# A graph kernel whose table entries are loaded as addresses without a range check at run time

## What is computed

```python
def reference(x, src, dst, edge_attr_4, edge_attr_8, ...):
    # layer 0: attention over the edges (4 heads of 64), plus one self-loop for each node
    h = (x @ W).reshape(N, H, C)
    e = leaky_relu(a_src[src] + a_dst[dst])
    alpha = exp(e - segment_max(e, dst)[dst]);  alpha /= segment_sum(alpha, dst)[dst]
    x = layernorm(x + elu(segment_sum(h[src] * alpha, dst) + bias + x @ skip_W))
    # layer 1: weights w from a three-layer MLP of edge_attr_8; reads at dst, sums into src
    w = mlp(edge_attr_8)                       # 256 values an edge
    mid_s, mid_v = products(w, ys[dst], yv[dst], edge_attr_4)
    ns, nv = segment_sum(mid_s, src), segment_sum(mid_v, src)   # scaled by rsqrt(degree)
    return layernorm(x + rms_normed(ns @ w2_s + sc_s, nv @ w2_v + sc_v))
```

## Time and profile before

| | |
|---|---|
| device time, median of 3 runs | 8239.94 us (8227.58 to 8246.67) |
| span of the profiled execution | 7531.3 us |
| device time of the profiled execution itself | not recorded; the timed median is 708.6 us above the span |
| TensorE busy (matmuls) | 6552.1 us, 87% |
| GpSimd busy | 5759.5 us, 76% |
| VectorE busy | 5437.6 us, 72% |
| ScalarE busy | 4022.4 us, 53% |
| mean granted TensorE clock | 0.988 |
| instructions, sequencers' among them | 218435 |
| instruction queues' DMA packets | 13 and 28 |

### The profile page before, as it was taken

The page is one execution under the profiler, slowest core; times in us unless marked ns, Lnnn a source line. Parts: engine busy times, 40 slices in busy tenths (PEclk is TensorE's granted clock), DMA queues, the critical chain, the costliest instruction groups (busy, mean ns, idle before and its releaser), DMA issues.

```text
span 7531.3 us, 218435 instructions
## 1 busy us (share of the span) xinstructions
PE 6552.1 (87%) x36547; PEld 4301.1 (57%) x36548; DVE 5437.6 (72%) x20339; ACT 4022.4 (53%) x12733; POOL 5759.5 (76%) x4888
## 2 busy tenths in 40 slices
PE   6999999999999988888888888888888888888876
PEld 5666666666666555555555555555555555555544
DVE  3788888888888798666666666666666666666668
ACT  2455555555555455555555555555555555555532
POOL 3677777777777655888888888888888888888878
PEclk8899999999999999999999999999999999999999
DMA  5788888888888766777777777777777777777789
GB/s 178 200 224 223 224 225 224 222 224 226 224 223 223 207 221 192 136 136 135 136 135 135 136 136 136 136 135 136 135 135 137 136 136 135 136 136 135 136 227 299
DMA packets 1268411, 1312.20 MB, mean 174 GB/s; under 512 B 232303, under 2 KB 1153040, under 8 KB 1268272
## 3 DMA queue, kind: packets, MB, share of 16 engines
q0 software_dynamic: 368112, 577.39, 45.5%
q1 hardware_dynamic: 900258, 734.36, 33.8%
HBM read 723.28 MB, written 587.78 MB: 174 GB/s over the span
## 4 chain that ended last, share of the span: by engine, by line
PE 38%; issue 23%; POOL 19%; DMA 8%; DVE 7%; POOLq 2%; ACT 2%; DVEq 1%; ACTq 0%; SPq 0%
POOL part L571 13%; PE PS L845 12%; PE PS L837 12%; DMA part<-arena,c_idx 8%; POOL d_out L562 5%; PE PS L866 3%; PE PS L862 2%; PE PS L959 2%; PE PS L952 1%; PE PS L878 1%; ACT arena L724 1%; DVE arena L1310 1%; PE PS L871 1%; PE PS L789 1%; DVE arena L1298 1%
## 5 line engine op out<-in xcount | busy, mean ns | idle before, releaser
L571 POOL DMA_INDIRECT part<-arena,c_idx x1664 | 2671.4, 1605 | 515.8 <-issue 457.7
L522 POOL DMA_INDIRECT arena<-h_tab,sidx x1664 | 1773.8, 1066 | 634.9 <-issue 385.7
L1279 DVE SCALAR_TENSOR_TENSOR arena<-PS,c_src,lower_eq 128x128 f32<-128x128 f32 x1664 | 517.6, 348 | 1385.1 <-PE PS L964 1385.1
L717 ACT COPY arena<-PS 128x514 f32<-128x514 f32 x832 | 489.7, 589 | 1823.5 <-DMA part<-arena,c_idx 1823.3
L952 PE MATMUL PS<-ident,arena 128*128 128x128 f32 x3328 | 545.1, 286 | 679.7 <-ACT arena L724 666.5
L921 PEld LDWEIGHTS PS<-ident,arena 128*128 128x128 f32 x6656 | 739.8, 141 | 626.9 <-issue 582.7
L562 POOL DMA_INDIRECT d_out<-y_tab,c_row x832 | 829.2, 997 | 266.6 <-issue 252.6
L921 PE MATMUL PS<-ident,arena 128*128 128x128 f32 x6656 | 977.0, 280 | 61.5 <-issue 43.0
L710 ACT COPY arena<-PS 128x512 f32<-128x512 f32 x1664 | 991.7, 603 | 6.8 <-PE PS L921 6.7
L1157 DVE TENSOR_TENSOR big<-big,PS 128x260 f32 x1664 | 703.9, 423 | 396.2 <-PE PS L845 336.1
L845 PE MATMUL PS<-arena 128*128 128x260 f32 x3328 | 961.4, 412 | 3.5 <-DVE big L1157 2.2
(11 more groups left out here) (192 smaller groups left out, 11545.7 us busy)
## 6 DMA issues: line engine op xcount, KB each, us to landing
w_tab<-arena SPq DMA_DIRECT2D x416, 520.0 KB
arena<-w_tab SPq DMA_DIRECT2D x1664, 130.0 KB
part<-zeros SPq DMA_DIRECT2D x1664, 32.1 KB
arena<-part SPq DMA_DIRECT2D x392, 128.5 KB, 3.4
arena<-h_tab,sidx POOLq DMA_INDIRECT x1664
ot_tab<-arena SPq DMA_DIRECT2D x416, 64.0 KB
arena<-ot_tab SPq DMA_DIRECT2D x416, 64.0 KB
part<-arena,c_idx POOLq DMA_INDIRECT x1664
```

The source lines that it names most:

```text
L522: pool.indirect_dma_start(hg[:, s, k, :], None, h_tab, bass.IndirectOffsetOnAxis(ap=sidx[:, s, k:k + 1], axis=0)).then_inc(s_hg[s], 16)
L571: pool.indirect_dma_start(part[q], bass.IndirectOffsetOnAxis(ap=c_idx[:, s, k:k + 1], axis=0), o_cmb[:, q, :], None, compute_op=ALU.add).t ...
```

## The change

`numbers` passes an argument that leaves out the run-time check of each loaded entry against its range. The two rows are clamped from below too, at 0, in the same two VectorE instructions that clamped them from above. Nothing else changes; the other loads with a range (the flag `wide`, and the entry in the loop that runs only where it is set) keep their checks.

```diff
+        IN_RANGE = "both rows are clamped to their range where they are built"
...
         def numbers(eng, row, at, n, below):
 
             return nc.values_load_multi_w_load_instructions(row[:, ds(at, n)], engines=(eng.engine,), min_val=0,
-                                                            max_val=below - 1)[1]
+                                                            max_val=below - 1,
+                                                            skip_runtime_bounds_check_because=IN_RANGE)[1]
...
             flat = PS[:, 0:4, :].rearrange("p b n -> p (b n)")[:, 0:T]
-            v.tensor_scalar(block_row, flat[0:1, :], float(NB - 1), None, ALU.min)
+            v.tensor_scalar(block_row, flat[0:1, :], float(NB - 1), 0.0, ALU.min, ALU.max)
             link(v.tensor_tensor(iota_t[32:33, :], flat[32:33, :], iota_t[32:33, :], ALU.add))
-            v.tensor_scalar(window_row, iota_t[32:33, :], float(EW - 1), None, ALU.min)
+            v.tensor_scalar(window_row, iota_t[32:33, :], float(EW - 1), 0.0, ALU.min, ALU.max)
```

## The result

The kernel after takes 8365.1 us (median of 4 runs, 8346.3 to 8392.6), the kernel before 8233.8 us on the same chip (4 runs, 8210.1 to 8246.7, the shown ones among them): a ratio of 1.017 with an interval of [1.0138, 1.0203]. It is slower, by some 131 us. The forecast was no change, 8239 us, and the range ended at 8275 us.

A forecast was written before the change was run, and what follows sets the result against it. The prediction took TensorE to bound stage A and GpSimd's scatters and gathers stage C. Its terms, four of 0, then -0.7 and +0.4, gave -0.3 us on 8239.94: 8239 us, range 8210 to 8275.

The forecast's parts named there:

- The sum: Whole kernel: all parts add to -0.3 us, set against the timed median 8239.94 us; the 708.6 us taken as untouched.
- Parts 1 and 2: Stage A: dropping TensorE's and VectorE's checks, 4 a step each, gains 0, as TensorE sets the pace.
- Part 2: Stage A, VectorE's 4 checks a step: 0.34 us idle before L1168, up to 141 us of room; gain 0.
- Part 3: Stage C, TensorE's checks in every second step: 0.28 us earlier, 116 us in all, then waiting for L724; gain 0.
- the rival priced at 116 us: Stage C: TensorE sets the pace, so 0.28 us comes out of each of 416 pairs, 8124 us; chance 0.07.
- the scatters get dearer: Stage C: SyncE's earlier loads raise one scatter in four to 1700 ns, +40 us, 8280 us; chance 0.08.
- Parts 4 and 5: SyncE's checks in stage C gain 0 directly; starts of stages A and C gain 0.7 us once, 0.5 at C.
- Part 6: The two clamps: a second operation costs 0 to 0.86 us once, taken as 0.4 us.

The follow-up runs named there:

- e16: Kernel before, unchanged, profiled in series 7 (late kind): 8213.1 us in one run, beside 8201.4 us for before.
- series 6: Late set of runs: before 8190.3 us; after with one added TensorE wait 8138.9 us (0.9949); after unchanged 8324.8 us (1.0162).
- e4: Kernel after, unchanged, run again in the prompt kind on another chip: 7526.0 us against 7529.9 us for before (1.0002).
- series 7: Late set of runs: before 8201.4 us; checks dropped only for TensorE's stage A loads 1.0054; checks kept only there 1.0177.
- series 4: Late set of runs: before 8261.4 us; after 0.9988; checks dropped only for TensorE's stage A loads 0.9958; kept only there 1.0003.
- e8: Kernel before, unchanged, in series 4 (late kind): before takes 8261.4 us there.
- e18: Kernel before with clamps and all checks dropped except those of TensorE's stage A loads, in series 7: 8381.6 us (1.0177).
- series 3: Late set of runs: before 8252.4 us; scatters cut to 64 of 128 rows, with checks 8036.0 us, without checks 7981.7 us.

## Why the prediction was wrong

**The step that failed is in "The sum":** "the 708.6 us between it and the timed median aren't in the trace, and nothing in the edit touches them." The 708.6 us aren't in that trace, but only because it shows another kind of execution; they were treated as time outside the span, and there is none: in every run since, the span is 1.6 to 3.0 us below the time of its own execution (8390.7 and 8392.55 for after). They were inside the timed executions, and there the edit does touch them. The terms for stage A were worked out from rows in which TensorE is never idle and at full clock, and were then applied to executions in which it is idle for 8 to 10% of the same 2200 us (183 us after, 226 in e16) at a mean clock of 0.85 and 0.94. In their place the runs show a stage A in which the time at the half clock varies between kernels and executions by hundreds of us, and that sets the time: 116 us of the 135 in series 6 by the estimate from the clock of the timed runs. 8.6% between span and time was the sign that was there to be read, ahead of any part. With the right kind of profile the parts would have been other ones; that they would have given a loss of 1.7% is not shown, since the way from the checks to the clock isn't.

**Parts 1 and 2, gain 0.** In the prompt kind they held. e4 in the stretch of the earlier trace rows:

```profile
300.00:2500.00 2200.00, 2200.00 (x10717) 1412.11 (x10715) 1805.98 (x6123) 1192.57 (x4596) 1633.91 (x1531) 1.00 0.83 224
3200.00:7100.00 3900.00, 3228.85 (x20567) 2145.34 (x20564) 2580.23 (x10666) 2226.32 (x6094) 3203.84 (x2286) 0.99 0.77 136
```

TensorE full, 10717 matmuls where there were 10718. VectorE's L1168, now L1170, starts without its idle time, as said. Its size was taken from a single step, though: from 300 to 2500 us the kernel before has 33.9 us of idle time before 383 of these instructions, in one of four, so that VectorE's room over the stage was some 37 us and not 141:

```profile
1504.07 0.25 DVE L1170 TENSOR_REDUCE ad<-PS 128x32 f32<-128x96 f32 x1
```

But "TensorE, which sets the pace, waits for none of it" fails in the late kind, where the third sum waits for L1157 (170 us in all in e16). The room that Part 2 gives to VectorE is there (L1168 some 0.5 us earlier in the step) and shortens no wait that matters; in series 7 the clock is low for longer with it, in series 4 not clearly. No rival had a TensorE that waits and a clock that falls in stage A; one of that form was missing, with the 708.6 us as its evidence.

**Part 3** held in its detail: L923 follows L933 by 1.01 us in a step without a load and in one with (e4):

```profile
5004.88 1.08 PE L933 MATMUL PS<-arena,w2m 128*64 128x128 f32 x8
5005.89 0.66 PE L923 MATMUL PS<-ident,arena 128*128 128x128 f32 x4
...
5011.16 1.08 PE L933 MATMUL PS<-arena,w2m 128*64 128x128 f32 x8
5012.17 1.09 PE L923 MATMUL PS<-ident,arena 128*128 128x128 f32 x8
```

and the wait behind it took the gain up: 660 us for L726 against 612, 48 more where I said some 100. The 0.28 us was again one step's. Over the 3900 us the kernel before has 55.1 us of idle time before L921 and e4 none before L923, so that the term, and with it the rival priced at 116 us, was twice too large. GpSimd stayed full with its own gap, 464.3 us before 1524 scatters of 1605 ns as in the earlier trace rows:

```profile
L573 POOL DMA_INDIRECT part<-arena,c_idx x1524 | 2446.1, 1605 | 464.3 <-issue 419.2 <-DVE arena L1322 38.1 <-DVE c_d L1318 5.8
L954 PE MATMUL PS<-ident,arena 128*128 128x128 f32 x3048 | 502.6, 288 | 671.2 <-ACT arena L726 660.4
```

**The rival "the scatters get dearer"** has its number in the result, 1675 ns after against 1605. It isn't what happened in the main: the kernel before has 1638 (e16) and 1674 (e8) in the late kind, and after has 1605 in the prompt one, so that the scatter goes mostly with the kind of execution. Read against the earlier trace rows alone, the result would have confirmed the wrong rival. A small part of it may be true. Within series 4 and 7 the kernels without SyncE's checks have the dearer scatters (1680 against 1638 and 1628 in series 7, 1683 and 1685 against 1674 and 1674 in series 4), and stage C of e18 is 31 us longer than that of e16; no run drops SyncE's checks alone. The rival's first price, 8280 us, also lay outside the range that was said to take in most of it, and 8239.6 us rounds to 8240.

**Parts 4 and 5.** Instructions fell from 218435 to 206787, 11648 as 5824 checks of two. SEQ_ASSERT is gone, one short FUSED_REGOPS for nearly each load stays. Line 318 in e4, and the start of stage C in its chain of waits:

```profile
L318 PEldq FUSED_REGOPS  x814: 42/46/60, 221.8 to 7175.5; - x163
L318 SPq FUSED_REGOPS  x820: 51/54/74, 2984.8 to 7176.5; - x164
L318 DVEq FUSED_REGOPS  x404: 53/53/82, 220.2 to 2537.4; - x135
```

```profile
2945.84 0.76 SPq L318
2946.77 0.37 SPq L449
```

0.93 us between the two starts against 1.49: 0.56 us saved, said was 0.5.

**Part 6** was put at 0.4 us. L1029 with its second operation takes 1018 ns, against 1016 without: nothing.

```profile
L1029 DVE TENSOR_SCALAR rows<-big x1: 1018/1018/1018, 33.2 to 33.2; 1x1664 int32<-1x1664 f32 x1
```

**The chances.** 0.08 for slower rested on one mechanism, in stage C. Four parts with a gain of 0 from hidden work looked like a safe case, while the one number that didn't fit, the 708.6 us, had no rival of its own. In the prompt kind the forecast of no change comes true, but the prediction was set against 8240 us and so was about the late kind.

**What stays open.** What makes the updates of TensorE's semaphores late in one series and prompt in another, on the same chip. How leaving out checks comes to more time at the lower clock, and whether it is VectorE's earlier start that does it, as series 7 suggests and series 4 doesn't. Kernels without checks have fewer instructions and other places in the program, which no run held apart from the checks. Why series 4, with a step of 6.66 instead of 6.79 us, shows no loss, and series 3 a gain. And whether all of the loss of the first result is VectorE's part: for that series there are only the two full kernels. No kernel here is the best in both kinds; the one with the stop is 0.5% faster than before where updates are late, and 1.05% slower where they are prompt.

## What to carry to other kernels

Before any row is read, set the profile's span beside the time of the runs it is to explain; here they were apart by 708.6 us where 1.6 to 3.0 us is the rule, because the profile was of another kind of execution, and a sum from its rows said nothing of the timed ones. A finding that work is hidden under a full engine holds for executions in which that engine is full: here two engines wait for each other in turn in the timed executions, the clock falls behind the gaps, and kernels that differ in checks of 0.3 us each were slower by 1.6 to 1.8% in three series of the late kind and not in the two others. Don't size a delay from one step; sum the idle time over the stretch. Compare kernels only with runs of the same series, and take a result of one series for what it is: the full edit gave 1.017, 1.0002, 0.9988, 1.0008 and 1.0162 in five.

## What was not expected of the hardware

- TensorE's semaphore updates can be held back: in late series those of up to four instructions came within 0.20 us of each other, 1.4 to 3.2 us after the start of their last matmuls, at the end of its stream of matmuls; in prompt series they came after 0.19 to 0.51 us. Two chips showed both kinds in different series, and all kernels of a series were of one kind, so that neither the chip nor the edit sets it.
- The granted clock fell to the lower level (0.50, 1.2 GHz) 21 to 36 times in stage A in late executions of kernels that differ in checks alone, and the time spent there, not the length of TensorE's waits, followed the time lost. It stayed low for tens of us with TensorE busy throughout (900 to 920 us of the kernel after).
- A scatter of 64 rows with addition takes 1476 ns in the late kind, one of 128 rows 1628 to 1685.
- The second operation of VectorE's clamp costs 2 ns in 1016.
